# A four-layer attention network on one core: q, k and v of self and cross attention as products of rounded parts, with the values and the output projection one unit later

## The reference, cut to what matters

```python
# layer 0, 16 heads of 16 features; mask 1 is one 64x64 mask, mask 2 is one per sequence
ln = layernorm(x, ln1_s, ln1_b)
q, k, v = jnp.split(ln @ w_qkv + b_qkv, 3, axis=-1)
x = x + merge_heads(attention(split_heads(q), split_heads(k), split_heads(v), mask1)) @ w_ao + b_ao
ln = layernorm(x, ln2_s, ln2_b)
q = ln @ w_q + b_q
k, v = jnp.split(ctx @ w_kv + b_kv, 2, axis=-1)          # ctx: 32 sequences of 64 tokens
x = x + merge_heads(attention(split_heads(q), split_heads(k), split_heads(v), mask2)) @ w_co + b_co
x = x + gelu(layernorm(x, ln3_s, ln3_b) @ w1 + b1) @ w2 + b2
# layer 1: a recurrent mixing layer; layer 2: two attentions over 16 heads of 128 features and an MLP
# layer 3: attention like the cross attention above (q from the norm, k and v from ctx), then an MLP
def attention(q, k, v, mask):
    s = jnp.einsum('bhqd,bhkd->bhqk', q, k) / sqrt(HD)
    s = s * mask - 10000.0 * (1.0 - mask)
    return jnp.einsum('bhqk,bhkd->bhqd', softmax(s), v)
```

## Time and profile before

| | |
|---|---|
| median of 3 runs (lowest, highest) | 1952.62 us (1952.59, 1954.22) |
| the profiled execution's own time | 1953.34 us |
| its span | 1951.5 us |
| PE busy | 1857.7 us (95%), 14320 records |
| DVE, ACT, POOL busy | 1112.3, 1043.3, 999.4 us |
| chain that ended last | PE 82%, DVE 9%, issue 4%, POOL 3%, ACT 2% |

### The profile page before, as it was taken

The page is one execution under the profiler, slowest core; times in us unless marked ns, Lnnn a source line. Parts: engine busy times, 40 slices in busy tenths (PEclk is TensorE's granted clock), DMA queues, the critical chain, the costliest instruction groups (busy, mean ns, idle before and its releaser), DMA issues.

```text
span 1951.5 us, 37701 instructions
## 1 busy us (share of the span) xinstructions
PE 1857.7 (95%) x14320; PEld 1506.0 (77%) x14320; DVE 1112.3 (57%) x2104; ACT 1043.3 (53%) x1945; POOL 999.4 (51%) x1140
## 2 busy tenths in 40 slices
PE   7999999989996999999999999999999998999899
PEld 5777779534454788888888888888888887967788
DVE  4566656489989555454544544544444445755654
ACT  3565543434344656665655656656665654345532
POOL 6776742366754544554544544545454535247620
PEclk9999999989998999999999999999999999999999
DMA  6000010000001222322322322322322310010000
GB/s 239 2 2 2 2 57 1 1 1 1 1 1 47 67 82 93 92 82 84 106 82 82 109 82 82 109 82 82 109 82 82 109 44 1 22 44 2 2 12 33
DMA packets 61842, 108.01 MB, mean 55 GB/s; under 512 B 7009, under 2 KB 42337, under 8 KB 60257
## 3 DMA queue, kind: packets, MB, share of 16 engines
q1 hardware_dynamic: 60784, 103.38, 17.1%
q10 hardware_dynamic: 880, 2.22, 0.3%
HBM read 103.47 MB, written 2.10 MB: 54 GB/s over the span
## 4 chain that ended last, share of the span: by engine, by line
PE 82%; DVE 9%; issue 4%; POOL 3%; ACT 2%; DMA 0%; DVEq 0%; SPq 0%; ACTq 0%; POOLq 0%
PE banks L867 18%; PE banks L938 9%; PE banks L895 9%; PE banks L632 7%; PE banks L649 7%; PE banks L927 6%; PE banks L471 6%; PE banks L908 3%; PE banks L480 3%; PE banks L553 2%; PE banks L528 2%; PE banks L510 2%; PE banks L539 2%; PE banks L916 1%; PE banks L465 1%
## 5 line engine op out<-in xcount | busy, mean ns | idle before, releaser
L1990 POOL TENSOR_TENSOR w_lo<-w2ring,w_hi 128x512 fp32r<-128x512 f32 x128 | 180.5, 1410 | 245.1 <-ACT w_hi L1133 245.1
L1812 DVE TENSOR_REDUCE nmax<-banks 128x4 f32<-128x260 f32 x128 | 54.2, 424 | 309.2 <-PE banks L908 309.2
L2073 POOL TENSOR_TENSOR wo_lo<-wo_ring,wo_hi 128x256 fp32r<-128x256 f32 x128 | 93.3, 738 | 250.7 <-ACT wo_hi L1341 250.5
L1800 DVE TENSOR_TENSOR v<-banks,dbv 128x512 f32<-128x512 f32 x128 | 88.6, 692 | 158.5 <-PE banks L895 158.5
L1341 ACT ACTIVATE wo_hi<-wo_ring 128x256 fp32r<-128x256 f32 x128 | 53.1, 417 | 190.6 <-PE banks L938 189.7
L938 PE MATMUL banks<-wo_hi,c_hi 128*128 128x256 f32 x512 | 148.8, 291 | 4.7 <-DVE c_lo L1805 4.4
L938 PE MATMUL banks<-wo_lo,c_hi 128*128 128x256 f32 x512 | 146.0, 285 | 0.0
L938 PE MATMUL banks<-wo_hi,c_lo 128*128 128x256 f32 x512 | 145.9, 285 | 0.0
L1328 ACT ACTIVATE k<-banks,cols 128x512 f32<-128x512 f32 x128 | 88.2, 689 | 80.4 <-PE banks L867 80.4
L927 PE MATMUL banks<-PT,v 128*128 128x128 f32 x1024 | 124.7, 275 | 1.0 <-issue 0.8
L927 PEld LDWEIGHTS banks<-PT,v 128*128 128x128 f32 x1024 | 119.7, 192 | 1.6 <-issue 1.2
(11 more groups left out here) (235 smaller groups left out, 5396.5 us busy)
## 6 DMA issues: line engine op xcount, KB each, us to landing
w2ring<-in_w SPq DMA_DIRECT2D x128, 384.0 KB, 3.2
b2ring<-in_b SPq DMA_DIRECT2D x128, 128.0 KB, 4.0
wo_ring<-in_wo SPq DMA_DIRECT2D x128, 128.0 KB, 3.2
mlp_w<-in_mlp SPq DMA_DIRECT2D x6, 1024.0 KB, 6.8
wl<-in_wres SPq DMA_DIRECT2D x1, 2688.0 KB, 8.7
X<-in_x_in SPq DMA_DIRECT2D x4, 512.0 KB, 11.2
wb<-in_wres SPq DMA_DIRECT2D x2, 1024.0 KB, 11.4
ctxT<-in_ctx_in SPq DMA_DIRECT2D x4, 512.0 KB, 19.5
```

The costliest lines, as they stand in the source:

```text
L1800: V.tensor_tensor(v2[i], held(("v2", v, i)).rearrange("p (s d) -> p s d", s=HV), dbv, ALU.add).then_inc(S["l2_v"], 1)
L1990: G.tensor_tensor(w2_lo[:, n % 2, :], w2ring[:, n % HR, 0:2 * KT * P], w2_hi[:, n % 2, :].bitcast(f32), ALU.subtract).then_inc(S["l2_wlo"], 1)
L2073: G.tensor_tensor(wo_lo[:, n % 2, :], wo_ring[:, n % WR, :], wo_hi[:, n % 2, :].bitcast(f32), ALU.subtract).then_inc(S["l2_wolo"], 1)
```

## The change

Chunks 1 to 7 of self and cross attention (`in_parts`) compute q, k and v as three products of rounded parts. Chunk 0 and the third attention stay in float32. ScalarE makes the high parts and VectorE the low parts: of the two weight sets (three pieces each, at the units that `weights_part_at` names), of the norm of the next chunk (p = 2), and of the context (ScalarE two chunks ahead at p = 2, VectorE one chunk ahead at p = 1). In all attention stages, the third too, TensorE's and VectorE's `values` move to chunk ai's own p = 1 (TensorE) and p = 2 (VectorE), `merge` to p = 2 and `update` to p = 3. Parts lie in memory that the second matrix of the first MLP is loaded into, so that load and the first users of other such places wait.

```diff
+def in_parts(ai):
+    return 0 < ai < 2 * CHUNKS
+def weights_part_at(ai, p):
+    return {(0, 0): (0, 0), (0, 1): (0, 1), (0, 2): (0, 2), (1, 0): (1, 0), (1, 1): (1, 1), (2, 0): (1, 2)}.get((ai, p))
 # TensorE
                     def source(ai, key):
+                        if in_parts(ai):
+                            pe.wait_ge(S["at_wlo"], 3 * (ai // CHUNKS + 1))
+                            if key and ai >= CHUNKS:
+                                pe.wait_ge(S["at_clo"], KT * (ai - CHUNKS + 1))
+                                return cs[c % 2]
+                            pe.wait_ge(S["at_hlo"], KT * ai)
+                            return ns
                     def project(ai, n, among):
+                        if in_parts(ai):
+                            src = source(ai, key)
+                            b = take(pe, ("qk", ai, n), "qk_T", 6 * ai + QK_DONE[n], among)
+                            pairs = [(x, y, k) for x, y in SPLIT for k in range(KT)]
+                            for x, y, k in pairs:
+                                last = mm(b, w[5][x][1 if key else 0][:, k, m * P:(m + 1) * P], src[y][:, k, :],
+                                          start=(x, y, k) == pairs[0], stop=(x, y, k) == pairs[-1])
...
-                    for g in range(2):
-                        values(start, g, among)
...
                         if p == 1:
                             for k in range(KT):
                                 front(attended(ai) + 1, k, among)
-                            if ai - 2 >= start:
-                                merge(ai - 2, among)
-                        if p == 2 and ai + 1 < stop:
                             for g in range(2):
-                                values(ai + 1, g, among)
+                                values(ai, g, among)
+                        if p == 2 and ai - 2 >= start:
+                            merge(ai - 2, among)
 # ScalarE, in the loop over units
+                        if weights_part_at(ai, p):
+                            weights_part_hi(*weights_part_at(ai, p))
+                        if p == 2:
+                            if in_parts(ai + 1):
+                                normed_hi(ai + 1)
+                            if CHUNKS <= ai + 2 < 2 * CHUNKS:
+                                attended_hi(ai + 2)
 # VectorE
+                    def normed_lo(ai):
+                        it = attended(ai)
+                        for k in range(KT):
+                            dve.wait_ge(S["at_hhi"], KT * (ai - 1) + k + 1)
+                            V.tensor_tensor(ns[1][:, k, :], hT2[:, it % 2, k, :], ns[0][:, k, :].bitcast(f32), ALU.subtract)\
+                                .then_inc(S["at_hlo"], 1)
...
                         scale(n)
-                        if p == 3 and ai + 1 < stop:
-                            if ai - 1 >= start:
-                                dve.wait_ge(S["att_pv"], n - LAG)
-                            values(ai + 1, 0)
+                        if p == 2:
+                            if ai - 2 >= start:
+                                dve.wait_ge(S["att_pv"], UNITS * (ai - 1))
+                            values(ai, 0)
                         if n > UNITS * start:
                             largest(n - 1)
-                        if p == 3 and ai + 1 < stop:
-                            values(ai + 1, 1)
+                        if p == 2:
+                            values(ai, 1)
                         if n - LAG - 1 >= UNITS * start:
                             weighed(n - LAG - 1)
-                        if p == 1 and ai - 2 >= start:
+                        if p == 3 and ai - 2 >= start:
                             update(attended(ai - 2))
+                        if weights_part_at(ai, p):
+                            weights_part_lo(*weights_part_at(ai, p))
+                        if p == 1 and CHUNKS <= ai + 1 < 2 * CHUNKS:
+                            attended_lo(ai + 1)
+                        if p == 2 and in_parts(ai + 1):
+                            normed_lo(ai + 1)
                         if p == 2 and ai + 1 == stop:
+                            if a0 == 0:
+                                dve.wait_ge(S["qk_mm"], 4 * stop)
+                                dve.wait_ge(S["v_mm"], 2 * stop)
                             split(it + 1)
 # SP
                 mlp_weights_up(0)
+                sp.wait_ge(S["qk_mm"], 4 * (2 * CHUNKS - 1))
+                sp.wait_ge(S["v_mm"], 2 * (2 * CHUNKS - 1))
                 mlp_weights_down(0)
```

More of the change, by code:

```diff
@@ L227, in build @@
                 for n, w in (("h_hi", 0), ("h_lo", 1024))]
+        cs = [[view(at(f"c_{n}_a{p}", w + 1024 * i, KT * TOK, f32r), "p (k n) -> p k n", k=KT) for i, n in enumerate(("hi", "lo"))]
+              for p, w in enumerate((M + 2048, A + 16640))]
+        ns = [hs_a[i][1] for i in range(2)]
+        NQ = 3 * KT * D
+        aw_raw = [wa[:, 0:NQ], wb[:, 0:NQ]]
+        aw_hi = [at(f"aw_hi{a}", A + 20736 + NQ * a, NQ, f32r) for a in range(2)]
+        aw_lo = [at(f"aw_lo{a}", w, NQ, f32r) for a, w in enumerate((A + 23808, WB))]
+        assert A + 23808 + NQ <= SIZE
         L1S, L1N = WAT["L1_m1"][0], WAT["L1_W"][0] + WAT["L1_W"][1] - WAT["L1_m1"][0]
@@ L508, in values @@
                             t = 2 * g + i
+                            if in_parts(ai):
+                                pairs = [(x, y, k) for x, y in SPLIT for k in range(KT)]
+                                for x, y, k in pairs:
+                                    last = mm(b[:, i * D:(i + 1) * D], src[x][:, k, t * P:(t + 1) * P], w[5][y][2][:, k, :],
+                                              start=(x, y, k) == pairs[0], stop=(x, y, k) == pairs[-1])
+                                continue
                             for k in range(KT):
@@ L987, in _, with by_k @@
                 kv = part(wb, "L0_q", "L0_kv")
+                def by_k(w):
+                    return view(w, "p (k n) -> p k n", k=KT)
+                own2 = [[by_k(x)[:, :, i * D:(i + 1) * D] for i in range(3)] for x in (aw_hi[0], aw_lo[0])]
+                cross2_w = [[by_k(x[:, 0:KT * D])] + [by_k(x[:, KT * D:])[:, :, i * D:(i + 1) * D] for i in range(2)]
+                            for x in (aw_hi[1], aw_lo[1])]
                 w3 = part(wb, "L3_qkv", "L3_qkv", 1)[:, 0, :].rearrange("p (w k n) -> p w k n", w=3, k=KT)
-                run([attention(0, [(own[:, :, 0:D], own[:, :, D:2 * D], own[:, :, 2 * D:3 * D], part(wa, "L0_qkv", "L0_ao"), s_w0),
-                                   (part(wb, "L0_q", "L0_q"), kv[:, :, 0:D], kv[:, :, D:2 * D], part(wb, "L0_q", "L0_co"), s_w1)]),
+                run([attention(0, [(own[:, :, 0:D], own[:, :, D:2 * D], own[:, :, 2 * D:3 * D], part(wa, "L0_qkv", "L0_ao"), s_w0, own2),
+                                   (part(wb, "L0_q", "L0_q"), kv[:, :, 0:D], kv[:, :, D:2 * D], part(wb, "L0_q", "L0_co"), s_w1, cross2_w)]),
                      mlp(0), rwkv(), cross2(), mlp(1),
@@ L1104, in mlp @@
                     act.wait_ge(S["mlp_in2"], 16 * (m + 1))
+                    if m == 0:
+                        act.wait_ge(S["qk_mm"], 4 * 2 * CHUNKS)
+                        act.wait_ge(S["v_mm"], 2 * 2 * CHUNKS)
                     for n in range(CHUNKS * MT):
@@ L1534, in weighed, with weights_part_lo, attended_lo @@
                             .then_inc(S["att_out"], 1)
+                    def weights_part_lo(a, i):
+                        dve.wait_ge(S["at_whi"], 3 * a + i + 1)
+                        third = slice(i * NQ // 3, (i + 1) * NQ // 3)
+                        V.tensor_tensor(aw_lo[a][:, third], aw_raw[a][:, third], aw_hi[a][:, third].bitcast(f32), ALU.subtract)\
+                            .then_inc(S["at_wlo"], 1)
+                    def normed_lo(ai):
+                        it = attended(ai)
+                        for k in range(KT):
+                            dve.wait_ge(S["at_hhi"], KT * (ai - 1) + k + 1)
+                            V.tensor_tensor(ns[1][:, k, :], hT2[:, it % 2, k, :], ns[0][:, k, :].bitcast(f32), ALU.subtract)\
+                                .then_inc(S["at_hlo"], 1)
+                    def attended_lo(ai):
+                        c = ai - CHUNKS
+                        for k in range(KT):
+                            dve.wait_ge(S["at_chi"], KT * c + k + 1)
+                            V.tensor_tensor(cs[c % 2][1][:, k, :], ctxT[:, c, k, :], cs[c % 2][0][:, k, :].bitcast(f32), ALU.subtract)\
+                                .then_inc(S["at_clo"], 1)
                     stats(attended(start) + 1)
                     dve.wait_ge(S["vbd_preset"], 1 if a0 == 0 else 2)
-                    for g in range(2):
-                        values(start, g)
                     for n in range(UNITS * start, UNITS * stop):
@@ L1592, in mlp @@
                         if i == 5 and c + 1 < CHUNKS:
+                            if m == 0 and c == 0:
```

(2 more changed lines are left out.)

25 lines of the change are left out of this document (23 added, 2 removed).

## The result

The changed kernel takes 1956.67 us (median of 20 runs, 1954.75 to 1958.56), the kernel before 1953.72 (20 runs, 1950.74 to 1957.97); the ratio is 1.0017 with a 95% interval of 1.0011 to 1.0024. It is slower by 0.11 to 0.24%, some 3 us, where 0.2% faster had been forecast. A second series of 11 runs gave 1.0015 [1.0007, 1.0024]. The profiled execution took 1955.69 us (span 1953.9): 2.35 more than before's 1953.34.

A forecast was written before the change was run, and what follows sets the result against it. TensorE's own work was taken to set the pace, the others having 8 to 12 us slack per chunk. Start 1.1, five chunks 1.8, end of cross 1.0 and third attention 0 sum to 3.9 us: 1948.7, range 1942 to 1957.

The forecast's parts named there:

- The start of the stage: Chunks 0 and 1: 1.4 us gained by the scores of chunk 1's p1, 0.3 given back after; net gain 1.1.
- 6 and 6 once: Making the weights' parts: 6 VectorE subtractions and 6 ScalarE copies, once, counted as added work on the other engines.
- the entry: Chunk 1's first projections wait for late norm's parts and run at low clock; scores of its p1 at 52.4, before 53.84.
- The steady chunk: Cross chunks: p0 to p3 take 6.74, 6.90, 7.61 and 7.43 us, 28.68 against 29.04; five chunks gain 1.8.
- the products in parts: TensorE's rounded matmuls: two projections take 2.78 us instead of 3.52, `values` 2.86 instead of 3.54.
- The p3 standstill: TensorE's second projection in p3 waits for the update of X to free a bank: new stall of 1.63 us.
- A: No p3 stall, the update being early enough; the matmul saving arrives whole: 13.2 us less, 1939.4; chance 0.13.
- VectorE's subtractions: Low parts of norm (p2) and context (p1): 0.69 us each alone, up to 1.22 beside GpSimd's work; norm's parts hidden.
- End of cross and third attention: Last cross chunk: output projection 1.0 us earlier against the chunk's start; third attention, reordered in float32, net 0.
- B: VectorE late: norm's subtractions take 1.22 us, `scale` in p3 comes 0.7 late in five chunks; 1952.2, no change; chance 0.16.
- C: Clock falls after the 1.63 us standstill in five chunks and the third stage, 6 x 1.85 us: 1959.8; chance 0.16.

The follow-up runs named there:

- pieces in chunks 1 and 2: Changed kernel with X's update ahead of `scale` in p3 and the weights' pieces in p1 of chunks 1 (one) and 2 (two): 1946.58 us.
- chunk 1 in float32: Changed kernel with chunk 1 kept in float32 like chunk 0, rounded parts beginning with chunk 2: 1954.56 us, ratio 1.0006 to the kernel before.
- order alone: Changed kernel with the new order but all q, k, v in float32 and no parts: 1952.99 us, ratio 1.0011 to the kernel before.

## Why the prediction was wrong

Its steps, forecast against trace, in us won (the forecast's first row is its 1.1 for the start and one chunk's 0.36):

| step | forecast | trace |
|---|---|---|
| up to the start of chunk 3 | 1.46 | -4.85 |
| chunk 3 to chunk 7, four periods | 1.44 | 0.27 |
| chunk 7 to the MLP stage | 1.0 | 1.24 |
| the rest, third attention in it | 0 | 0.94 |
| sum | 3.9 | -2.4 |

**The start of the stage is the step that failed.** The forecast followed VectorE through chunk 0 with care and named the piece of the weights there. For chunks 1 and 2 it said of the weights only "6 and 6 once" under work that is hidden. It priced the instructions and not the wait in front of them: VectorE works through its list in order (at 55.34 `scale` stands behind the piece), and ScalarE's half of the piece stands behind a normalisation that waits for GpSimd. Moving the pieces took 1.9 us off each of the two places, 3.8 of the 6.3 us that this step is off. p1 of chunk 1 itself was at 51.86, even ahead of the 52.4 forecast, so the entry (the norm's parts late, cold projections) was judged right. The other part is p3 of chunk 1, where TensorE waits 2.03 us for the norm's parts; the forecast had the wait and not the low clock after it, which costs 1.6 (9.72 us from p3 to chunk 2 against 8.12 where the clock held). With the pieces in p1 and the clock up, chunk 2 began at 72.06; the forecast had 71.6. In that trace p1 to p3 of chunk 1 still took 20.4 us, 1.2 more than the forecast's 19.2, and what is left of the 6.3 beyond that is 0.3 in chunk 2, less the 0.5 won at p1. No run splits the 1.2.

**The steady chunk** was right in kind: period 28.97 for 28.68, `weigh` of p2 released by `vbd`, p2 7.60 for 7.61, p3 7.50 for 7.43. One term was mis-sized, the products in parts, from rows of the MLP stage: two projections take 3.10 us (109.32 to 112.42), not 2.78, and `values` 3.05 (116.34 to 119.39), not 2.86. That makes p0 6.91 and not 6.74. The p3 standstill ends 4.88 us after p3's scores (which are at 99.07), forecast 4.98, and is 1.36 long instead of 1.63, mostly because the projection ahead of it is longer. Moving the update removed it, which shows its cause; whether A or the forecast came hung on one line's place in VectorE's list.

**VectorE's subtractions.** In p2 the norm's parts take 0.64 each, the forecast's 0.69. The context's in p1 take 1.39 to 2.39, more than the 1.22 kept. Below is their duration over all eight (ns min/median/max), and what stood beside the pair at 117.53 on GpSimd:

```profile
L1637 DVE TENSOR_TENSOR c_lo_a<-ctxT,c_hi_a x8: 1385/1894/2387, 117.5 to 205.7; 128x512 fp32r<-128x512 f32 x8
```
```profile
113.21 1.90 POOL L2035 TENSOR_TENSOR T<-T,nmax 128x1024 f32<-128x1024 f32 x1
...
115.94 2.43 POOL L2030 TENSOR_TENSOR T<-T,a_self 128x1024 f32<-128x1024 f32 x1 [0.83 <-DVE T L1600]
118.32 2.37 POOL L2035 TENSOR_TENSOR T<-T,nmax 128x1024 f32<-128x1024 f32 x1
120.65 2.81 POOL L2004 TENSOR_TENSOR X<-X,rows 128x1024 f32<-128x1024 f32 x1
```

The rows fit one behind the other. The first subtraction begins at 117.53 and takes 1.39 us: it ends 0.55 after GpSimd's mask addition (118.37). The second takes 2.39 and ends at 121.23, 0.54 after GpSimd's subtraction of the maximum (120.69). GpSimd waits in the same way: that subtraction takes 2.37 instead of the 1.90 at 113.21, and the bias addition 2.81 instead of the 2.36 of the one at 91.18. The Trainium skill, "SBUF — State Buffer", section "SBUF: two separate sides", has the two exclude each other for whole instructions. The trace agrees: each waits for what is left of the other's instruction and then takes about its usual time. This costs the pair 2.4 us (3.70 less 1.29). It is more than the 1.15 that the forecast kept (twice 1.22, less 1.29) and less than two whole mask additions of 2.36, because the first one was met with 0.84 us left. The forecast had the size wrong and its consequence right: `scale` of p2 at 121.61 waits 0.38 us for the scores, so the slack of p1 was just enough. It was not when the third piece of the weights (3.1 to 3.3 us) or `vbd` (1.0 to 3.5 us a chunk) was put into this unit too.

**End of cross and third attention.** 35.74 us from chunk 7 to `merge` of chunk 6 instead of 36.98, so 1.24 for 1.0. The distance to before is 2.9 us at the first projection of the third attention and 2.4 at the end, so 0.5 for 0 with the last MLP behind it, within its bounds; the other 0.4 went between 711 us and there.

**The rivals.** A did not come with the order as it was. B did not come: in p3 `scale` waits for the scores (0.42 us at 129.21). C did not come in the steady chunks: the clock is 1.00 from 100 to 220 us with a standstill of 1.36 in each. It came at 70 us, in a place that it did not name. Its condition, a limit between standstills of 1.64 and 1.73 us, is not borne out (last section): the length alone did not settle it. The range ended at 1957, the time is 1956.7.

## What to carry to other kernels

When preparatory work is spread over the idle places of an in-order engine, price the wait for its input and name what is queued behind it, not only its own duration. The engine's total slack (8 to 12 us a chunk here) says nothing about one slot: p1 had 0.4 us left. And where a wait for a bank appears, look for the instruction that frees it and ask if it can stand a few places earlier; one moved call was worth 6 us, twice what the change lost.

## What the runs showed of the hardware

The clock after a standstill of about 2 us is not settled by the program. The same kernel, in two executions, TensorE's order of time, first one and then the other, each with its granted clock:

```profile
70.02 0.70 PE L534 MATMUL banks<-h_hi_a,aw_hi 128*128 128x512 f32 x2 [2.03 <-issue]
70.56 0.84 PE L534 MATMUL banks<-h_lo_a,aw_hi 128*128 128x512 f32 x2
71.19 1.05 PE L534 MATMUL banks<-h_hi_a,aw_lo 128*128 128x512 f32 x2
```
```profile
70.00:80.00 10.00, 9.98 (x99) 8.07 (x100) 7.40 (x16) 5.70 (x8) 6.19 (x3) 0.83 0.01 2
```
```profile
71.97 0.47 PE L534 MATMUL banks<-h_hi_a,aw_hi 128*128 128x512 f32 x1 [2.03 <-issue]
```
```profile
70.00:80.00 10.00, 8.03 (x98) 6.80 (x98) 9.23 (x20) 6.62 (x9) 6.32 (x4) 1.00 0.01 2
```

In the first the level falls from 2.4 to 1.2 GHz and costs 1.6 us, in the second it stays. Eight traces have this standstill of 2.02 or 2.03 us, and five of them show the fall. The length of the standstill just ahead does not order the cases either: in the steady chunks none came after 1.36 us and three of four after 3.4, none after 1.79 us (94.88, pieces in chunks 1 and 2), both times after 2.39. Twice it came at work, over 1 us after a standstill of only 1.11 us had ended, at 67 us with chunk 1 in float32 and in the order alone:

```profile
61.61 1.97 PE L582 MATMUL banks<-consts,T 128*128 128x128 f32 x8
63.37 4.22 PE L491 MATMUL banks<-hT,wa 128*128 128x512 f32 x8
```

The runs of one kernel spread over 3.8 us (changed kernel) to 9.7 us (order alone), more than the whole change moved; a fall at such a place is worth 1.6 us here and 1.7 at 361 us, but the runs' spread was not traced to it one by one.
